# A decoder kernel with two attentions and two expert mixtures: the vector engine's first fills in 24 pieces, and one sum moved to GpSimd

## The chip, the cores and the metric

One Trainium2 chip, one of its cores. The metric is the device time of one execution in microseconds; for the kernel before it is the median of three. A core has five engines that run their own instruction streams and meet at semaphores: TensorE (PE; its weight loads are shown as PEld), the vector engine (DVE), the scalar engine (ACT), GpSimd (POOL), and SyncE (SP), which here only issues DMAs.

## The reference

The input x is 32 batches of 256 tokens by 128 channels, float32. The result is x + A(xn) + F(xn), where xn is x normalised over its channels.

```python
xn = _layernorm(x, axis=-1)
# A: attention with 16 heads of 8, rotary angles, a distance decay, causal softmax, output projection
# F: a second block on the same xn:
n1 = _layernorm(xn, ln1_w, ln1_b)
rw = _gating(n1, smha_sim, smha_gates, 2)            # 8 experts
q, k, v = einsum('btc,ech,bte->bth', n1, {q,k,v}_proj, rw)
attn_out = einsum('bth,ehc,bte->btc', softmax(q k^T / sqrt(128)) v, o_proj, rw)
hs = xn + attn_out
n2 = _layernorm(hs, ln2_w, ln2_b)
rw2 = _gating(n2, moe_sim, moe_gates, 2)
F = hs + einsum('btei,eic,bte->btc', gelu(einsum('btc,eci->btei', n2, w1)), w2, rw2)
```

What matters for the change: at the end the sum x + A + hs of a batch, called the base, is added to the second mixture's output.

## The kernel before, in words

Work is software-pipelined over the 32 batches. `step(n, u, n_x)` is written out once for every engine and holds that engine's share of step n: the second pass of attention for batch n, the maxima of batch n+1, the projections and gating of batch n+2, the first normalisation of batch n+3. `u` is the parity of n, for double buffers; `n_x` is 3 in full steps and falls to 2, 1, 0 at the end, where stages run out. Steps 0 and 1 are unrolled, then a hardware loop (`Fori(1, NB // 2 - 2)`, L1397 on DVE) runs 13 times over two steps, steps 2 to 27, and steps 28 to 31 are unrolled again. Every engine has its own loop of this kind (L517 SP, L663 POOL, L960 ACT, L1397 DVE, L1853 PE); there is no barrier between iterations, only semaphores. After step 31 a second stage follows, the mixture of `w1` and `w2` over all tokens (L1406 and after on DVE).

The order on each engine is written by hand. On DVE a step begins with `next_max(1)` (`row_max`, L1210: a row maximum over two PSUM banks, which also frees these banks for TensorE's next `unit1`), then the first two instructions of `layer_norm(n + 3)` (L1018, two `bn_stats`), a drain (L1019) and `bn_aggr` (L1021). The gating's chain of small operations follows, with more maxima between its links, then `scale_att` (L1261), `add_x` (L1268, writes `xa`), `rotate` (L1125 to L1137), and at the very end `add_hs`:

```python
                ins.then_inc(hs_done, 1)
                dve.wait_ge(hs_done, n + 1)
                dve.wait_ge(xa_done, n + 1)

                dve.wait_ge(base_stored, 16 * n)
                dve.tensor_tensor(bs[:, u], hv, xa[:, u], ALU.add).then_inc(base_done, 1)
```

Here `hs` is updated by two `scalar_tensor_tensor` (L1277) and the base is summed (L1284). SP's step n+1 begins with `wait_ge(base_done, n + 1)`, stores the base to DRAM (L474), loads `xr` for the next `add_x` (L470), spreads the gating weights (L464), and issues 24 `stk` loads (L447) and others. POOL's step holds `second_norm(n + 3)` (L643, L647), which waits for the normalisation's chain in DVE's step, and `scale(n + 1)` (L636, eight products), which waits for `max_parts` in DVE's step (L1224).

Before all this DVE writes constants: seven `memset` (L1060 to L1068), each counted on the semaphore `set_dve`. `N_FILL` is their number; SP, ACT and PE wait for that count (L414, L683, L817), and the normalisation of batch 0 follows on DVE once its x has come.

An engine's instructions stand in DRAM and are brought to it by DMA. The compiled program has 64 bytes for an instruction. Register, wait and branch instructions are among them, and count where places in the stream are given below. DVE's stream of this kernel has 437 instructions ahead of its loop (the engine's start-up apart), and the loop's body has 352. ACT's body has 107, SP's 98, POOL's 36, PE's about 1230. These counts are of the instruction records; no view prints them.

Of the kernel before, what the change touches and what calls it, by code (L numbers as in the profile page):

```python
# [10 lines left out]
ALU = mybir.AluOpType  # L11
# [4 lines left out]
S = 256  # L16
# [3 lines left out]
P = 128  # L20
T = S // P
# [104 lines left out]
def build(nc, x, w_attn, w_o, log_xi, pi_logit, e_logit, ln1_w, ln1_b, ln2_w, ln2_b, sim1, gates1,  # L126
# [9 lines left out]
    with ExitStack() as ctx:  # L136
        def sb(name, shape, dt=F32):
            return ctx.enter_context(nc.sbuf_tensor(name, shape, dt))

        def sem(name):  # L140
            return ctx.enter_context(nc.semaphore(name))
# [20 lines left out]
        ones_p = sb("ones_p", [P, P])  # L162
# [42 lines left out]
        mpart = sb("mpart", [P, T, P], BF16)  # L205
# [12 lines left out]
        hs = sb("hs", [P, NB * T, D])  # L218
        bs = sb("bs", [P, 2, T, D])
        xa = sb("xa", [P, 2, T, D])  # L220
# [85 lines left out]
        xa_done = sem("xa_done")  # L306
# [13 lines left out]
        hs_done = sem("hs_done")  # L320
        base_done = sem("base_done")
        base_stored = sem("base_stored")
# [26 lines left out]
        block = ctx.enter_context(nc.Block())  # L349
        N_CONST, N_W, N_SMALL = 8, 5, 4  # L350
        N_ROWS = 2 * NF + 2 * NF
        N_FILL = 7
        SIN_READY, N_SET_DVE = N_FILL + 11, N_FILL + 12
        UP, MOE = (2, 5, 0, 1), (4, 3)

# [22 lines left out]
        def _(sp_):  # L378
# [34 lines left out]

            sp_.wait_ge(set_dve, N_FILL)  # L414
            sp_.wait_ge(set_pool, 1)
# [175 lines left out]
        @block.gpsimd  # L591
        def _(pool):
            flat = stk[:].rearrange("p a s h t -> p a s (h t)").bitcast(F32)
            pool.memset(flat[:, 0, 0], 0.0).then_inc(set_pool, 1)
            pool.memset(flat[:, 0, 1], BF16_ONES).then_inc(set_pool, 1)
            pool.wait_ge(upper_made, 1)
            for f in range(NF):
                pool.memset(vst[:].rearrange("p a i (f g) r -> p (a i) f g r", f=NF)
                            [:, :, f, :, VO[f] + DH:VO[f] + DH + 1], 1.0).then_inc(set_pool, 1)

            def bias_rows():

                c = Chain(pool, bias_chain, 0, BIAS_LINKS)
                pool.wait_ge(ld_const, 16 * N_CONST)
                pool.wait_ge(set_act, 4)
                c.link(pool.tensor_scalar(bias_in[:, 1:2], bias_in[:, 1:2], 0.5, 0.5, ALU.mult, ALU.add))
                c.link(pool.tensor_tensor(bias_in[:, 0:1], bias_in[:, 0:1], bias_in[:, 1:2], ALU.mult))
                c.link(pool.tensor_scalar(cb[:, 0], cpos[:], bias_in[:, 0:1], None, ALU.mult))
                c.link(pool.tensor_scalar(cb[:, 1], cb[:, 0], -1.0, None, ALU.mult))
                for part in range(3):  # L610
                    c.link(pool.tensor_copy(cbp[:, :, part], cb[:]))
                    if part < 2:
                        c.link(pool.tensor_tensor(cb[:], cb[:], cbp[:, :, part], ALU.subtract))
                c.close()

            def masks():

                c = Chain(pool, mask_made, 0, 5)
                pool.wait_ge(ld_half, 16 * 4 * NF)
                for k, by in ((2, NEAR / BIG), (3, FAR / BIG), (1, FAINT)):  # L620
                    c.add(pool.tensor_scalar(mask_half[:, k], mask_half[:, k], by, None, ALU.mult))
                c.wait()
                c.add(pool.tensor_tensor(mask_r[:], mask_half[:, 3:4].broadcast_to((P, HG, P)),
                                         mask_half[:, 2:3].broadcast_to((P, HG, P)), ALU.add))
                c.add(pool.tensor_tensor(mask_l[:], mask_half[:, 1], mask_half[:, 0], ALU.add))
                c.close()

            def scale(b, par):

                pool.wait_ge(rep_in, 16 * (b + 1))  # L630
                pool.wait_ge(n1T_done, b + 1)
                pool.wait_ge(ve_out, b)
                if not isinstance(b, int) or b:
                    pool.wait_ge(max_chain, (MAX_LINKS + 1) * (b + 1))
                for e in range(E):
                    pool.tensor_tensor(n1s[:, e], rep[:, par, e], n1T[:, par], ALU.mult).then_inc(n1s_done, 1)  # L636

            def second_norm(b):

                pool.wait_ge(ln_chain, LN1_LINKS * (b + 1))  # L640
                pool.wait_ge(ln_out, b + 1)
                pool.wait_ge(xzT_out, b)
                pool.tensor_tensor(zt[:], xn[:],  # L643
                                   rstd[:, 1, 0:T].rearrange("p (i o) -> p i o", o=1).broadcast_to((P, T, D)),
                                   ALU.mult).then_inc(zp_done, 1)
                hv = hs[:, T * b:T * b + T] if isinstance(b, int) else hs[:, bass.ds(b * T, T)]
                pool.tensor_copy(hv, xn[:]).then_inc(keep_done, 1)  # L647

            def step(n, u, n_x):
                if n_x == 3:  # L650
                    second_norm(n + 3)
                if n_x:
                    scale(n + 1, 1 - u)

            second_norm(0)
            bias_rows()
            masks()
            second_norm(1)
            scale(0, 0)
            second_norm(2)  # L660
            step(0, 0, 3)
            step(1, 1, 3)
            with pool.Fori(1, NB // 2 - 2) as j:  # L663
                for u in range(2):
                    step(2 * j + u, u, 3)
            step(NB - 4, 0, 3)
            step(NB - 3, 1, 2)
            step(NB - 2, 0, 1)
            step(NB - 1, 1, 0)
# [3 lines left out]
        def _(act):  # L673
# [8 lines left out]
            act.activation(pig[:], pig[:], ACT.Tanh, scale=0.5).then_inc(set_act, 1)  # L682
            act.wait_ge(set_dve, N_FILL)  # L683
            ones = ones_p[:].rearrange("p (o t) -> p o t", o=1)
# [322 lines left out]
        def _(dve):  # L1007
# [49 lines left out]
                c.close()  # L1057

            ch = Chain(dve, set_dve, 0, N_SET_DVE)
            ch.add(dve.memset(ones_p[:], 1.0))  # L1060
            ch.add(dve.memset(ones_b[:], 1.0))
            ch.add(dve.memset(zeros_b[:], 0.0))
            ch.add(dve.memset(simx[:], 0.0))
            ch.add(dve.memset(ones_e[:], 1.0))
            ch.add(dve.memset(mpart[:], 0.0))

            ch.wait()
            ch.link(dve.memset(simx[:, 2, E:E + 1], 1.0))  # L1068
            assert ch.k == N_FILL, ch.k
            ROUND = 1.5 * 2.0 ** 23  # L1070
# [200 lines left out]
            def add_hs(n, u):  # L1271
                dve.wait_ge(oe_out, n + 1)
                dve.wait_ge(keep_done, n + 1)
                hv = hs[:, T * n:T * n + T] if isinstance(n, int) else hs[:, bass.ds(n * T, T)]
                dve.wait_ge(snorm_chain, n + 1)
                for i in range(T):
                    ins = dve.scalar_tensor_tensor(hv[:, i], ps[:, G1, i * D:(i + 1) * D], smx[:, 3, i:i + 1],  # L1277
                                                   hv[:, i], ALU.mult, ALU.add)
                ins.then_inc(hs_done, 1)
                dve.wait_ge(hs_done, n + 1)  # L1280
                dve.wait_ge(xa_done, n + 1)

                dve.wait_ge(base_stored, 16 * n)
                dve.tensor_tensor(bs[:, u], hv, xa[:, u], ALU.add).then_inc(base_done, 1)  # L1284

            def layer_norm2(g):

# [30 lines left out]
            def step(n, u, n_x):  # L1318
# [41 lines left out]
                if n_x >= 2:  # L1360
                    row_max(n + 2, 0)
                run(turn)
                add_hs(n, u)

            dve.wait_ge(set_act, 7)
# [97 lines left out]
        def _(pe):  # L1463
# [7 lines left out]
            def norm_T(b, banks, free):  # L1471

                free()
                pe.wait_ge(ln_out, b + 1)
                pe.wait_ge(zp_done, b + 1)
                for k, src in enumerate((xn[:], zt[:])):
                    for i in range(T):
                        ins = pe.transpose(ps[:, banks[0], (T * k + i) * P:(T * k + i + 1) * P], src[:, i], ident[:])
                ins.then_inc(xzT_out, 1)
# [336 lines left out]
            norm_T(0, FIRST, lambda: None)  # L1816
            pe.wait_ge(set_dve, N_FILL)
            pe.wait_ge(sim_chain, 1)
# [141 lines left out]
```

## Time and profile before

| | us |
|---|---|
| median of 3 runs (lowest, highest) | 1325.96 (1323.41, 1326.18) |
| the profiled execution | 1324.63 |
| its span | 1322.7 |
| PE busy | 1203.3 (91%) |
| DVE busy | 1034.0 (78%) |
| ACT busy | 718.8 (54%) |
| POOL busy | 222.4 (17%) |

The span is what the profile covers; 1.9 us of the execution's time lie around it. Busy times leave out waits and register instructions. "issue" in the chain of waits and as a releaser is time in which an engine waited for nothing that the profile shows.

### The profile page before, as it was taken

The page shows a single profiled execution, that of the slowest core. Times are in us where ns is not written, and L with a number is a line of the kernel's source. Part 1 is how long each engine was busy: PE and PEld are TensorE (multiplying, and loading weights), DVE is VectorE, ACT ScalarE, POOL GpSimd, SP SyncE. Part 2 cuts the span into 40 slices and gives each one's busy share as a digit, 9 for nine tenths or more (in the row PEclk, how much of TensorE's full clock was granted, in tenths as well). Part 3 has the DMA queues.
Part 4 walks back from the last instruction along what each step waited for, and adds up shares of the span by engine and source line. Part 5 has one row for each costly group of instructions (what it writes and reads, how often), then busy time and mean ns, then how long its engine had stood idle before and what let it go on. Part 6 is the DMA issues. An engine that isn't in the chain of part 4 may idle for free.

```text
span 1322.7 us, 33146 instructions
## 1 busy us (share of the span) xinstructions
PE 1203.3 (91%) x10652; PEld 917.5 (69%) x10652; DVE 1034.0 (78%) x3697; ACT 718.8 (54%) x1292; POOL 222.4 (17%) x342
## 2 busy tenths in 40 slices
PE   2599989898989898989898979898999989999998
PEld 1377767676767676767676757676787767777776
DVE  8899969696969696969696969696997577777664
ACT  4166646464646464646464646464656865555532
POOL 4112111111111111111111211121231100000000
PEclk9899989897989897989898989898999999999999
DMA  4533322322222222222222222222233144444453
GB/s 106 147 107 107 91 87 81 83 81 82 80 83 82 82 82 82 80 84 82 82 81 82 82 81 82 82 82 82 83 93 91 38 149 161 161 161 161 162 195 140
DMA packets 103172, 133.50 MB, mean 101 GB/s; under 512 B 13576, under 2 KB 82424, under 8 KB 94864
## 3 DMA queue, kind: packets, MB, share of 16 engines
q1 hardware_dynamic: 100548, 130.72, 31.9%
q10 hardware_dynamic: 2508, 1.58, 0.5%
q14 instruction: 85, 0.70, 0.2%
q8 instruction: 31, 0.51, 0.2%
HBM read 109.12 MB, written 21.54 MB: 99 GB/s over the span
## 4 chain that ended last, share of the span: by engine, by line
PE 52%; DVE 27%; issue 17%; DVEq 2%; ACT 1%; DMA 1%; ACTq 1%; POOL 0%; SPq 0%; POOLq 0%
PE ps L1890 8%; PE ps L1876 8%; PE ps L1613 5%; PE ps L1623 4%; PE ps L1659 4%; PE ps L1614 4%; DVE mx L1210 3%; PE ps L1590 3%; PE ps L1486 2%; DVE rots L1129 2%; PE ps L1539 1%; PE ps L1549 1%; PE ps L1573 1%; DVE rots L1126 1%; DVE rots L1135 1%
## 5 line engine op out<-in xcount | busy, mean ns | idle before, releaser
L1210 DVE TENSOR_REDUCE mx<-ps 128x4 f32<-128x1024 f32 (+1 forms) x192 | 234.9, 1223 | 80.0 <-PE ps L1549 33.1
L779 ACT ACTIVATE pr<-ps 128x1024 f32<-128x1024 f32 x192 | 196.6, 1024 | 170.3 <-PE ps L1573 104.4
L636 POOL TENSOR_TENSOR n1s<-rep,n1T 128x256 f32<-128x256 f32 x256 | 177.3, 730 | 323.8 <-DVE mpart L1224 307.1
L785 ACT ACTIVATE ps<-trn 128x1024 f32<-128x1024 bf16 x191 | 196.5, 1029 | 5.1
L1613 PE MATMUL ps<-n1s,wqk 128*128 128x256 f32 x512 | 180.0, 436 | 0.0
L1890 PEld LDWEIGHTS ps<-w2s,ats 128*128 128x128 f32 x1024 | 131.4, 191 | 52.7 <-issue 43.9
L1614 PE MATMUL ps<-n1s,wqk 128*128 128x256 f32 x512 | 166.3, 409 | 0.0
L979 ACT ACTIVATE n1s<-ps 128x512 f32<-128x512 f32 x128 | 76.6, 598 | 121.0 <-PE ps L1876 119.9
L1890 PE MATMUL ps<-w2s,ats 128*128 128x128 f32 x1024 | 136.0, 276 | 2.4 <-DVE ats L1414 2.4
L1623 PE MATMUL ps<-wv,n1s 128*128 128x128 f32 x1024 | 133.1, 278 | 0.0
L1876 PE MATMUL ps<-rep,w1s 128*128 128x512 f32 x256 | 130.7, 594 | 0.0
L1623 PEld LDWEIGHTS ps<-wv,n1s 128*128 128x128 f32 x1024 | 124.3, 192 | 4.9
L1659 PE MATMUL ps<-wop,ats 128*128 128x128 f32 x1024 | 126.4, 276 | 0.0
L1659 PEld LDWEIGHTS ps<-wop,ats 128*128 128x128 f32 x1024 | 119.6, 192 | 5.6 <-issue 2.9
L1614 PEld LDWEIGHTS ps<-n1s,wqk 128*128 128x128 f32 x512 | 107.0, 209 | 17.6
L1613 PEld LDWEIGHTS ps<-n1s,wqk 128*128 128x128 f32 x512 | 96.5, 210 | 28.4 <-issue 18.0
L643 POOL TENSOR_TENSOR zt<-xn,rstd 128x256 f32<-128x256 f32 x32 | 20.5, 642 | 492.6 <-DVE rstd L1038 492.6
L1261 DVE TENSOR_TENSOR ats<-rep,ps 128x512 f32<-128x512 f32 (+1 forms) x160 | 81.1, 572 | 0.0
L732 ACT ACTIVATE n1T<-xzT,lnp 128x256 f32<-128x256 f32 x32 | 19.2, 600 | 110.3 <-POOL n1s L636 110.3
L1590 PE MATMUL ps<-pr,vst 128*32 128x256 f32 x1024 | 74.2, 411 | 0.6 <-ACT pr L779 0.6
L1539 PE MATMUL ps<-mask_r,mask_l 64*128 64x256 bf16 x256 | 37.2, 287 | 40.5 <-DVE mx L1210 40.5
L1539 PEld LDWEIGHTS ps<-mask_r,mask_l 64*128 64x128 bf16 x256 | 12.3, 93 | 71.0 <-DVE mx L1210 54.3
(229 smaller groups left out, 2074.9 us busy)
## 6 DMA issues: line engine op xcount, KB each, us to landing
rep<-scr_rw SPq DMA_DIRECT2D x32, 1024.0 KB, 5.7
stk<-scr_rw SPq DMA_DIRECT2D x16, 1024.0 KB, 8.6
scr_parts<-parts SPq DMA_DIRECT2D x64, 192.0 KB, 5.8
stk<-scr_parts SPq DMA_DIRECT2D x248, 48.0 KB
rots<-scr_rw SPq DMA_DIRECT2D x8, 1024.0 KB, 4.7
wqk<-scr_rw SPq DMA_DIRECT2D x8, 1024.0 KB, 9.1
stk<-scr_parts SPq DMA_DIRECT2D x248, 32.0 KB
xt<-in_x SPq DMA_DIRECT2D x32, 128.0 KB, 2.2
```

Source lines behind the costliest of these rows:

```text
L636: pool.tensor_tensor(n1s[:, e], rep[:, par, e], n1T[:, par], ALU.mult).then_inc(n1s_done, 1)
L779: act.activation(pr[:, Q, :, i], ps[:, S2[0]:S2[0] + NF], ACT.Exp).then_inc(exp_done, 1)
L785: act.activation(ps[:, S2[0]:S2[0] + NF], seeds[:, kind:kind + 1].broadcast_to((P, NF, 512)), ACT.Copy).then_inc(seed_done, 1)
L1210: dve.tensor_reduce(mx[:, min(i, 1)].rearrange("p (f h) -> p f h", f=NF)[:, :, h:h + n], ps[:, S1[0]:S1[0] + NF].rearrange("p f (h t) -> p ...
L1261: dve.tensor_tensor(ats[:, e:e + ne], rep[:, u, e:e + ne], ps[:, G0:G0 + 1, 0:S].broadcast_to((P, ne, S)), ALU.mult).then_inc(ats_done, 1)
L1590: mm(ps[32 * h:32 * h + 32, PVB, 0:S], vst[:, u, 0, HH * f + HG * Q + h], pr[:, Q, f, h // 2, (h % 2) * S:(h % 2 + 1) * S], start=(f == 0) ...
L1613: mm(ps[:, QKB, 0:S], wq[:, e], n1s[:, e], start=(e == 0), stop=(e == E - 1), skip_group_check=True)
L1614: ins = mm(ps[:, QKB, S:2 * S], wk[:, e], n1s[:, e], start=False, stop=(e == E - 1), skip_group_check=True)
L1623: ins = mm(ps[:, QKB, i * D:(i + 1) * D], n1s[:, e, i * P:(i + 1) * P], wv[:, e], start=(e == 0 and i == 0), stop=(e == E - 1), skip_group ...
L1659: ins = mm(ps[:, G1, i * D:(i + 1) * D], ats[:, e, i * P:(i + 1) * P], wop[:, e], start=(e == 0 and i == 0), stop=(e == E - 1), skip_group ...
L1876: mm(ps[:, UP[k % 4]], w1s[:, e], n2T[t % 8], start=True, stop=True).then_inc(up_out, 1)
L1890: ins = mm(ps[:, MOE[t % 2], i * D:(i + 1) * D], hgs[:, k % 2, i * P:(i + 1) * P], w2s[:, e], start=(e == 0 and i == 0), stop=(e == E - 1) ...
```

## The change

The fill of `ones_p` becomes 16 `memset` of 8 columns each, that of `mpart` 8 `memset` of 32 elements a row each, so that `N_FILL` is 29 in place of 7. The base's sum leaves DVE's `add_hs` and becomes `add_base` at the end of GpSimd's step, with the same three waits. What is computed stays the same. In the words that came with it, DVE's loop then begins at instruction 455 of its stream.

```diff
-        N_FILL = 7
+        FILLS_ONES, FILLS_MAX = 16, 8
+        N_FILL = 5 + FILLS_ONES + FILLS_MAX
...
+            def add_base(n, u):
+
+                pool.wait_ge(hs_done, n + 1)
+                pool.wait_ge(xa_done, n + 1)
+                pool.wait_ge(base_stored, 16 * n)
+                hv = hs[:, T * n:T * n + T] if isinstance(n, int) else hs[:, bass.ds(n * T, T)]
+                pool.tensor_tensor(bs[:, u], hv, xa[:, u], ALU.add).then_inc(base_done, 1)
+
             def step(n, u, n_x):
                 if n_x == 3:
                     second_norm(n + 3)
                 if n_x:
                     scale(n + 1, 1 - u)
+                add_base(n, u)
...
-            ch.add(dve.memset(ones_p[:], 1.0))
+            for k in range(FILLS_ONES):
+                ch.add(dve.memset(ones_p[:, k * P // FILLS_ONES:(k + 1) * P // FILLS_ONES], 1.0))
             ch.add(dve.memset(ones_b[:], 1.0))
             ch.add(dve.memset(zeros_b[:], 0.0))
             ch.add(dve.memset(simx[:], 0.0))
             ch.add(dve.memset(ones_e[:], 1.0))
-            ch.add(dve.memset(mpart[:], 0.0))
+            mparts = mpart[:].rearrange("p i h -> p (i h)")
+            for k in range(FILLS_MAX):
+                ch.add(dve.memset(mparts[:, k * S // FILLS_MAX:(k + 1) * S // FILLS_MAX], 0.0))
...
                 ins.then_inc(hs_done, 1)
-                dve.wait_ge(hs_done, n + 1)
-                dve.wait_ge(xa_done, n + 1)
-
-                dve.wait_ge(base_stored, 16 * n)
-                dve.tensor_tensor(bs[:, u], hv, xa[:, u], ALU.add).then_inc(base_done, 1)
```

## Rows read from the trace of the kernel before

**Rows 1.** The page: span; chain by engine; instruction DMA queues (packets, MB).
```profile
span 1322.7 us, 33146 instructions
...
q14 instruction: 85, 0.70, 0.2%
q8 instruction: 31, 0.51, 0.2%
...
PE 52%; DVE 27%; issue 17%; DVEq 2%; ACT 1%; DMA 1%; ACTq 1%; POOL 0%; SPq 0%; POOLq 0%
```

**Rows 2.** DVE's waits: line, releaser: us in total, times, longest.
```profile
DVE bmv L1021 <- issue: 52.6, 12, 4.8
...
DVE mx L1210 <- issue: 32.5, 12, 3.0
```

**Rows 3.** The chain of waits across one back jump of DVE's loop: start, us, what.
```profile
640.63 0.06 DVEq L1397
640.69 2.76 issue
643.45 0.09 DVEq L1397
...
644.73 0.47 DVE bst L1018 x2
645.20 3.97 issue
649.18 0.16 DVEq L1019
```

**Rows 4.** DVE's loop instruction: all its branches.
```profile
L1397 DVEq COMPARE_BRANCH  x13: 55/63/72, 179.2 to 969.2; - x13
```

**Rows 5.** Steps by window, the odd ones' sum last: us, busy PE, PEld, DVE, ACT, POOL, PEclk.
```profile
122.20:150.88 28.68, 28.41 (x286) 22.59 (x285) 26.11 (x94) 18.61 (x33) 6.51 (x10) 1.00 0.34 96
150.88:179.14 28.26, 27.84 (x282) 21.85 (x281) 26.11 (x94) 17.54 (x33) 6.49 (x10) 1.00 0.35 96
...
640.54:677.50 36.96, 31.63 (x285) 24.25 (x284) 26.28 (x95) 18.57 (x33) 6.52 (x10) 0.91 0.26 73
677.50:705.76 28.26, 27.84 (x283) 21.97 (x282) 26.26 (x95) 17.69 (x33) 6.49 (x10) 1.00 0.35 95
...
sum 450.86, PE 383.19 PEld 292.57 DVE 315.87 ACT 223.30 POOL 78.42; mean PE 31.93 PEld 24.38 DVE 26.32 ACT 18.61 POOL 6.54
```

**Rows 6.** Instruction DMAs in windows 122.2:179.1 (two rows), 640.5:706, 640.5:643.5 and 645.2:649.4.
```profile
q8 instruction: 5, 0.08, 0.6%
q14 instruction: 5, 0.04, 0.3%
...
q14 instruction: 5, 0.04, 0.2%
...
q14 instruction: 1, 0.01, 1.0%
...
q14 instruction: 1, 0.01, 0.5%
```

**Rows 7.** DVE in order of time at the end of a step without a jump.
```profile
676.76 0.61 DVE L1277 SCALAR_TENSOR_TENSOR hs<-ps,smx,hs 128x128 f32 x2
677.50 0.42 DVE L1284 TENSOR_TENSOR bs<-hs,xa 128x256 f32<-128x256 f32 x1
677.84 1.22 DVE L1210 TENSOR_REDUCE mx<-ps 128x4 f32<-128x1024 f32 x1
```

**Rows 8.** PE in order of time: waits for that maximum; then slow after a jump.
```profile
679.11 0.28 PE L1539 MATMUL ps<-mask_r,mask_l 64*128 64x256 bf16 x2 [0.31 <-DVE mx L1210]
...
644.87 0.28 PE L1539 MATMUL ps<-mask_r,mask_l 64*128 64x256 bf16 x2 [2.70 <-DVE mx L1210]
...
645.81 1.22 PE L1613 MATMUL ps<-n1s,wqk 128*128 128x256 f32 x2
```

**Rows 9.** GpSimd's product, and two equal DVE products, the first beside it.
```profile
L636 POOL TENSOR_TENSOR n1s<-rep,n1T 128x256 f32<-128x256 f32 x256 | 177.3, 730 | 323.8 <-DVE mpart L1224 307.1 <-DMA rep<-scr_rw 16.8
...
L1129 DVE TENSOR_TENSOR rots<-rots,cs 128x512 f32<-128x512 f32 x32 | 30.8, 963 | 1.1
L1130 DVE TENSOR_TENSOR rots<-rots 128x512 f32<-128x512 f32 x32 | 22.1, 692 | 1.1
```

**Rows 10.** SP's and GpSimd's waits in the window 677.5 to 706.
```profile
SPq L474 <- DVE bs L1284: 8.0, 1, 8.0
...
POOL zt L643 <- DVE rstd L1038: 13.5, 1, 13.5
```

**Rows 11.** DVE's first instructions in order of time.
```profile
0.82 0.17 DVE L1060 MEMSET ones_p<- 128x128 f32 x1 [0.82 <-PEq L1954]
...
1.45 0.07 DVE L1064 MEMSET ones_e<- 128x8 f32 x1
1.49 0.17 DVE L1065 MEMSET mpart<- 128x128 uint32 x1
...
3.05 0.48 DVE L1018 BATCH_NORM_STATS2 bst<-xt 128x6 f32<-128x128 f32 x2 [1.27 <-DMA xt<-in_x]
```

## The prediction

> **What bounds the kernel now.** I read the page first: TensorE and DVE carry the chain, but 17% of it is "issue", time in which nothing is shown to be waited for [rows 1]. The view of DVE's waits puts this in one place. The `bn_aggr` of the first normalisation and the maximum `mx` wait for "issue" 12 times each, 52.6 and 32.5 us [rows 2]. DVE's loop branches 13 times and jumps back 12 times [rows 4]. The chain of waits across one jump shows both: after the branch 2.76 us of nothing, the maximum and two `bn_stats`, then 3.97 us of nothing before the drain [rows 3].
>
> The steps fall into two kinds [rows 5]. The 12 that begin with a jump take 450.86 us together, 37.57 each; the others of the same form take 28.26. The difference, 9.31 us, is 6.7 us of the two gaps and the rest TensorE's: it waits 2.70 us for the maximum and then runs a pair of products in 1.22 us where it takes about 0.6 otherwise [rows 8], and the granted clock of such a step is 0.91 against 1.00 [rows 5], a part of it at 1.2 in place of 2.4 GHz.
>
> The gaps are instruction fetches. In each a packet of an instruction queue starts, and five come in the 65 us of an iteration [rows 6]; 85 packets are 0.70 MB [rows 1], so a packet is 8 KB, at 64 bytes 128 instructions. The body of 352 instructions needs 3 to 4 such blocks; five packets an iteration mean that all of it, and the block after it, is fetched anew each time.
>
> **Where the block's edges are.** The second gap stands before the drain, the eighth instruction of the body. With 437 ahead of the loop an edge lies after 444 of them, the next at 572, 700 and 828. The body before, 437 to 788, so touches four blocks, 7 instructions in the first. Entering a block starts the fetch of the next (in straight stretches packets come once per 128 instructions, with no gap). So five are wanted in one turn, and when DVE jumps back the first is gone.
>
> How many are kept? The first turn, window 122.2 to 179.1, has 5 packets on q14 and 5 on q8, which is TensorE's with 16 KB each [rows 1, 6]. By count 3 of the 5 on q14 are DVE's, one each ACT's and SP's, whose bodies of 107 and 98 have an edge inside. In a later turn q8 has none and q14 only DVE's five [rows 6]. ACT and SP thus keep at least 3 blocks of 8 KB (two touched, one ahead), and TensorE, whose body touches six, at least 7 of 16 KB. DVE fails with 5. The case of 4 is not shown.
>
> **The change part by part.** *The place.* 24 fills stand for 2, which is 22 more; the two unrolled steps ahead of the loop lose the sum and one wait instruction each, 4 fewer: 437 + 22 - 4 = 455, as the change says. The body has at most 352, so it lies in 455 to 806, between the edges 444 and 828, with 11 and 22 to spare: three blocks and one ahead, 4 in all. I take it that four are kept, since an engine that keeps three and fails at five sits by a power of two at four, and because TensorE keeps seven or more of the larger. Then no jump fetches, and a step with a jump is as long as one without. Steps 1, 2 and 3 ran in sequence with no jump between them in 28.68 and 28.26 us [rows 5], so the 28.26 is no catching-up after a stall. The gain is 450.86 - 12 x 28.26 = 111.7 us. Bounds: nothing, and 111.7.
>
> *The sum's removal from DVE.* In a step without a jump the sum starts at 677.50 and the next maximum at 677.84; the last `hs` update ends at 677.37 [rows 7]. DVE's queue is shorter by 0.47 us a step. TensorE, though, is busy 27.84 of 28.26 us, and waits for DVE's maximum 0.31 us [rows 5, 8]. It has no more to give: of the 0.47, 0.31 a step, over 29 steps 9.0 us. What is late next is TensorE's own stream. In the last three steps DVE is not the one waited for. Bounds: 0, and 29 x 0.47 = 13.6 us.
>
> *The sum on GpSimd.* No row shows this operation there. The nearest is its product of two operands of the same 128x256, 0.73 us [rows 9]. It runs after `scale`, when the next work of that engine is 13.5 us away behind the normalisation [rows 10], so nothing queues behind it: `second_norm(n + 4)` and `scale(n + 2)` both wait for DVE's next step. The store of the base comes about 0.4 us later, and with it in SP's queue the `xr` load, the weights' spread and the `stk` loads. SP waits 8.0 us there in a full step [rows 10], which hides it. Cost 0; without that cover 0.4 x 31 = 12 us. The other price is DVE beside GpSimd: its product L1129 takes 0.963 us on average, the equal L1130, with GpSimd quiet, 0.692 [rows 9]. The sum would run beside the maximum and `bn_stats`; I take 0, with 0.27 x 31 = 8 us as the upper bound, and 0 below.
> The Trainium skill ("SBUF — State Buffer", section "SBUF: two separate sides") has a DVE operation with two SBUF inputs locked out for the whole of a GpSimd operation. L1129 agrees in direction. By that rule an overlap with such an operation would cost 0.73 us a step, 23 us in all; the maximum (from PSUM) and `bn_stats` have one input, and by the same rule go free.
>
> *The fills.* The narrowest fill seen, 8 columns, took 0.07 us, the wide ones 0.17 [rows 11]. 24 at 0.07 to 0.17 are 1.7 to 4.1 us in place of 0.33. The x of batch 0 leaves 1.27 us idle before the first `bn_stats` [rows 11], so at 0.08 each (nearest to the narrow row) it is 1.9 - 0.3 - 1.3, some 0.3 us late; ACT's clearing of `vst`, which waits for the count, may follow. I take 1 us; bounds 0 and 3.
>
> *Sum*, against the profiled execution's 1324.63 (span 1322.7 and 1.9 around it): 1324.6 - 111.7 - 9.0 + 0 + 1.0 = 1204.9. The median of the runs is 1.3 above that execution, so 1206; with half of the unknown delays beside GpSimd (2 us) I forecast 1208.
>
> **The rivals.** *A: fewer than four blocks are kept.* The jump still misses, but the next block is fetched during the 117 instructions that remain in the first. The gap of 3.97 goes with what follows it; the first gap stays, 2.70 us of TensorE's wait and some 1.6 us of slow products after it. Per jump 4.3 in place of 9.31, 12 x 5.0 = 60 us: 1324.6 - 60 - 9 + 1 + 1.3 = 1258. For it: the four is not shown. Against: it would leave three. Chance 0.07.
> The Trainium skill ("Runtime: NRT & Kernel Launch", section "Instruction fetch mechanics") speaks for A: only two lines of 16 KB, and a taken branch out of them stops for a fetch. Here q14's packets are 8 KB and come one by one, and ACT keeps three, so the trace does not bear out its size of line; its total of 32 KB would be four of 8 KB, which is my forecast.
>
> *B: after a jump that misses, the next block is asked for only when the stream reaches the edge.* Then, if A's condition holds too, the gap of 3.97 just moves 117 instructions on: 1324.6 - 9 + 1 + 1.3 = 1318. For it: the second packet starts after DVE has stopped at the drain. Against: edges elsewhere cost nothing. Chance 0.05.
>
> *C: the base comes too late for SP* (slower). Place: L474, at the head of SP's step. Price 0.4 to 0.5 us a step, 14 us over 31, if SP's wait of 8.0 us were used up; it counts as slower only where the jumps keep their price: 1326 + 14 = 1340. Against: that wait. Chance 0.02.
>
> *D: the change doesn't do what it says*: the edges lie elsewhere than I count and the body still has four blocks and a short first one, DVE's shorter queue alone remaining and eaten by GpSimd's sum: about 1325. Against: the drain's place and 455 agree to the instruction. Chance 0.02.
>
> **How the numbers follow.** The forecast has 0.84. Its own range: low 1196 with DVE's full 0.47 a step and no cost for the fills (1326.0 - 111.7 - 13.6 = 1200.7, and 5 for products that follow sooner), high 1225 with TensorE's 0.31 not gained and 8 us beside GpSimd (1326.0 - 111.7 + 8 + 3). It holds 19 of 20 of that case, 0.80 in all, so it reaches to no rival. Faster by over 0.2% (2.7 us, about what a measurement of this kernel can tell from no change): the forecast, A and B, 0.96. Within 0.2%: D, 0.02. Slower: C, 0.02.
>
> **What would show it.** Right: no "issue" rows at the head of the loop for L1210 and L1021; no q14 packets in the middle of the loop and about 60 fewer than 85 in all; every full step near 28.0 us at a clock of 1.00; TensorE's wait for `mx` gone from steps of both kinds; a GpSimd `bs` of 0.6 to 0.8 us; L474 waiting for it with several us left. Wrong: five q14 packets an iteration still and one gap at the branch (A); a second gap some 117 instructions after the jump (B); DMAs of `stk` awaited by TensorE (C). Should steps stay at 28.26 without jumps' gaps, then only the term of 9 us was wrong.

## The result and the profile after

| | before | after |
|---|---|---|
| median of 4 runs on one chip, us (lowest, highest) | 1326.07 (1323.41, 1329.04) | 1211.95 (1211.61, 1212.19) |
| ratio, with its 95% interval | 1 | 0.9139 [0.9119, 0.9158] |
| span of the profiled execution, us | 1322.7 | 1210.4 |
| granted clock, mean of that execution | 0.958 | 0.994 |

The kernel is 114 us faster, 8.6%. The forecast of 1208 was 4 us short of it, and 1211.95 lies in its range.

The page of the kernel after: span, busy time, two instruction queues, and the chain that ended last. It answers to [rows 1].

```profile
span 1210.4 us, 33207 instructions
...
PE 1161.8 (96%) x10652; PEld 896.3 (74%) x10652; DVE 1018.8 (84%) x3687; ACT 717.7 (59%) x1292; POOL 245.9 (20%) x374
...
q8 instruction: 31, 0.51, 0.2%
q14 instruction: 26, 0.21, 0.1%
...
PE 77%; DVE 14%; issue 6%; ACT 1%; ACTq 1%; DVEq 1%; DMA 1%; POOL 0%; SPq 0%; POOLq 0%
```

Queue q14 carries 26 packets in place of 85, q8 (TensorE's) the same 31 as before. "issue" falls from 17% of the chain to 6%, and TensorE holds 77% of it in place of 52%. DVE's largest waits (line, releaser: us in total, times, longest) now all name TensorE; the two "issue" rows of [rows 2] are gone.

```profile
DVE ats L1422 <- PE ps L1898: 66.4, 73, 2.3
DVE mx L1223 <- PE ps L1557: 20.7, 36, 1.7
DVE xa L1281 <- PE ps L1681: 16.1, 29, 0.6
```

The loop still runs 13 times and jumps back 12 times, as in [rows 4]:

```profile
L1405 DVEq COMPARE_BRANCH  x13: 50/56/67, 178.1 to 855.5; - x13
```

DVE in order of time across the jump at 403.91 (start, us, instruction), to set beside [rows 3]. The maximum follows the last `hs` update at once, and the `bn_aggr` follows `bn_stats`: neither gap is left.

```profile
404.05 0.60 DVE L1290 SCALAR_TENSOR_TENSOR hs<-ps,smx,hs 128x128 f32 x2
404.56 1.22 DVE L1223 TENSOR_REDUCE mx<-ps 128x4 f32<-128x1024 f32 x1
405.69 0.47 DVE L1028 BATCH_NORM_STATS2 bst<-xt 128x6 f32<-128x128 f32 x2
406.24 0.25 DVE L1031 BATCH_NORM_AGGREGATE bmv<-bst 128x2 f32<-128x6 f32 x2
```

Three steps by window, from one end of `hs` to the next, the first with that jump (columns as in [rows 5]). A step with a jump is as long as one without, at a clock of 1.00, and TensorE is busy for all but 0.11 to 0.13 us of it. TensorE's waits for DVE's maximum, 40.5 us in 29 cases and 33.9 in 13 before, are 2.8 in 4 and 2.6 in one.

```profile
404.91:433.15 28.24, 28.11 (x284) 22.30 (x283) 25.53 (x94) 18.16 (x33) 7.26 (x11) 1.00 0.33 95
433.15:461.36 28.21, 28.10 (x284) 22.27 (x283) 25.92 (x94) 18.05 (x33) 7.24 (x12) 1.00 0.33 95
461.36:489.57 28.21, 28.09 (x284) 22.23 (x283) 25.48 (x94) 18.10 (x33) 7.26 (x12) 1.00 0.33 95
```

From the ends of `hs` in both traces the difference closes. The first comes 0.4 us later (93.99, 94.39). The 12 steps with a jump take 338.7 us in place of 449.7, and the 19 others together 2.4 us less. What follows the last is 0.7 us longer (245.5, 246.2). 0.4 - 111.0 - 2.4 + 0.7 = -112.3, which is the difference of the spans.

### The profile page after: what moved, and what is told of

It is laid out like the page before. It is cut to its first block, busy times and chain, and to the rows that moved or that the text cites. A ratio compares the mean times of both kernels' runs of the same rounds, so it can differ in the third digit from the quotient of the medians.

```text
span 1210.4 us, 33207 instructions
## 1 busy us (share of the span) xinstructions
PE 1161.8 (96%) x10652; PEld 896.3 (74%) x10652; DVE 1018.8 (84%) x3687; ACT 717.7 (59%) x1292; POOL 245.9 (20%) x374
## 4 chain that ended last, share of the span: by engine, by line
PE 77%; DVE 14%; issue 6%; ACT 1%; ACTq 1%; DVEq 1%; DMA 1%; POOL 0%; SPq 0%; POOLq 0%
PE ps L1621 10%; PE ps L1667 10%; PE ps L1898 9%; PE ps L1622 9%; PE ps L1884 9%; PE ps L1631 5%; PE ps L1494 3%; PE ps L1598 3%; PE ps L1581 2%; PE ps L1557 2%; PE ps L1547 2%; PE ps L1544 2%; DVE att L1249 1%; PE ps L1554 1%; PE ps L1603 1%
## 5 line engine op out<-in xcount | busy, mean ns | idle before, releaser
L1621 PE MATMUL ps<-n1s,wqk 128*128 128x256 f32 x512 | 164.7, 404 | 1.3 <-issue 1.3
L1622 PE MATMUL ps<-n1s,wqk 128*128 128x256 f32 x512 | 153.8, 382 | 0.0
L1622 PEld LDWEIGHTS ps<-n1s,wqk 128*128 128x128 f32 x512 | 98.4, 192 | 13.8
L1621 PEld LDWEIGHTS ps<-n1s,wqk 128*128 128x128 f32 x512 | 89.3, 195 | 26.0 <-issue 15.9
L742 ACT ACTIVATE n1T<-xzT,lnp 128x256 f32<-128x256 f32 x32 | 19.2, 600 | 108.2 <-POOL n1s L637 108.2
L1598 PE MATMUL ps<-pr,vst 128*32 128x256 f32 x1024 | 68.5, 385 | 0.6 <-ACT pr L789 0.6
L656 POOL TENSOR_TENSOR bs<-hs,xa 128x256 f32<-128x256 f32 x32 | 23.3, 728 | 200.2 <-DVE hs L1290 200.2
L1422 DVE TENSOR_TENSOR ats<-n1s,stk 128x512 f32<-128x512 f32 x64 | 44.0, 688 | 14.0 <-PE ps L1898 13.9
```

The lines of the kernel that those rows point to most:

```text
L1598: mm(ps[32 * h:32 * h + 32, PVB, 0:S], vst[:, u, 0, HH * f + HG * Q + h], pr[:, Q, f, h // 2, (h % 2) * S:(h % 2 + 1) * S], start=(f == 0) ...
L1621: mm(ps[:, QKB, 0:S], wq[:, e], n1s[:, e], start=(e == 0), stop=(e == E - 1), skip_group_check=True)
L1622: ins = mm(ps[:, QKB, S:2 * S], wk[:, e], n1s[:, e], start=False, stop=(e == E - 1), skip_group_check=True)
```

## The experiments

All runs stand in one table; ratios are against runs of the kernel before on the same chip. "Left" is how many instructions of the body lie in the block it begins in, by edges after 444, 572, 700 and 828. "Second packet" is when, after a branch that misses, the second instruction packet starts, as a mean over 12 jumps; it is from the trace's packet records, which no view prints. Steps run from one end of `hs` to the next, means over the loop without its first step. A blank means that it does not apply.

| run | sum on | loop, first to last | left | q14 | second packet, us | step with jump | other | median, us | ratio [95%] |
|---|---|---|---|---|---|---|---|---|---|
| before | DVE | 437-788 | 7 | 85 | 7.12 | 37.48 | 28.36 | 1326.07 | 1 |
| after | GpSimd | 455-801 | | 26 | none | 28.23 | 28.20 | 1211.95 | 0.9139 [0.9119, 0.9158] |
| fills_only | DVE | 459-810 | | 26 | none | 28.48 | 28.36 | 1217.85 | 0.9175 [0.9156, 0.9195] |
| sum_only | GpSimd | 433-779 | 11 | 85 | 3.58 | 30.99 | 28.22 | 1246.97 | 0.9399 [0.9374, 0.9424] |
| head_437 | GpSimd | 437-783 | 7 | 85 | 3.71 | 31.71 | 27.97 | 1251.12 | 0.9441 [0.9416, 0.9466] |
| head_443 | GpSimd | 443-789 | 1 | 85 | 3.71 | 35.40 | 27.94 | 1295.41 | 0.9753 [0.9726, 0.9779] |
| head_444 | GpSimd | 444-790 | | 25 | none | 28.34 | 28.09 | 1211.66 | 0.9129 [0.9106, 0.9152] |
| head_481 | GpSimd | 481-827 | | 26 | none | 28.22 | 28.22 | 1212.08 | 0.9139 [0.9117, 0.9161] |
| head_483 | GpSimd | 483-829 | 89 | 86 | (text) | 32.57 | 28.23 | 1264.21 | 0.9530 [0.9504, 0.9556] |
| dve_443 | DVE | 443-794 | 1 | 86 | 7.16 | 39.87 | 28.35 | 1354.20 | 1.0214 [1.0189, 1.0239] |
| rep_late | DVE | 437-788 | 7 | 85 | 4.03 | 32.85 | 28.35 | 1269.50 | 0.9586 [0.9564, 0.9608] |
| rep_sooner | GpSimd | 437-783 | 7 | 85 | 7.10 | 36.95 | 27.97 | 1314.44 | 0.9931 [0.9908, 0.9954] |
| pe_less | GpSimd | as after | | 26 | none | 28.21 | 28.17 | 1211.13 | 0.9153 [0.9131, 0.9174] |
| seven_experts | GpSimd | as after | | 26 | none | 27.93 | 27.93 | 1204.72 | 0.9085 [0.907, 0.910] |

### The two parts apart

fills_only takes the fills of the change and leaves the sum on DVE (against the kernel before, the fills' loops as in the change):

```diff
-        N_FILL = 7
+        FILLS_ONES, FILLS_MAX = 16, 8
+        N_FILL = 5 + FILLS_ONES + FILLS_MAX
```

> The 24 fills alone, the base's sum left on DVE: DVE's loop then begins after 459 instructions and its 352 end at 810, three blocks. Theory W (DVE keeps four blocks of 128 instructions, the one fetched ahead included, edges after 444, 572, 700 and 828): no fetch in the loop, steps of 28.2 to 28.3 us, 1212 to 1214 us, the whole gain. Theory S (the sum's move carries a part of the gain worth the forecast's 9 us): 1219 to 1222 us, steps of 28.5 us. A theory that the gain is the sum's alone would have 1326 us.

sum_only takes the sum's move and leaves the fills whole (on the kernel after):

```diff
-        FILLS_ONES, FILLS_MAX = 16, 8
+        FILLS_ONES, FILLS_MAX = 1, 1
```

> The sum on GpSimd alone, the seven fills as before: the loop begins after 433 and ends at 779, four blocks, 11 instructions in the first. Theory W: five packets an iteration as before, a first gap of 2.6 to 3 us at the jump and a second of 4 us some 11 instructions on; 1323 to 1327 us. Theory S: 1317 us, since DVE's queue is 0.47 us a step shorter.

The fills alone bring 108.2 us, to 1217.85, and all gaps are gone (109.4 us by the ratio to the kernel before in the same set of runs). Behind them the sum's move is worth another 5.9 us (4.8 by the ratios). The second run was the surprise. With the loop at 433, in the wrong place, its queue has 85 packets as before, and yet it takes 1247, not about 1326; neither theory had that. Its page and DVE's waits:

```profile
q14 instruction: 85, 0.70, 0.2%
...
DVE mx L1223 <- issue: 27.1, 12, 2.4
```

The gap at the branch is still there (before: 32.5). The row for `bn_aggr`, 52.6 us in [rows 2], is not. Both parts therefore work against the same loss, and their gains don't add: 108 and 79 alone, 114 together.

### Where the edges are

All four on the kernel after, and only the number of fills differs:

```diff
-        FILLS_ONES, FILLS_MAX = 16, 8
+        FILLS_ONES, FILLS_MAX = 8, 4      # head_443
+        FILLS_ONES, FILLS_MAX = 8, 5      # head_444
+        FILLS_ONES, FILLS_MAX = 40, 10    # head_481
+        FILLS_ONES, FILLS_MAX = 40, 12    # head_483
```

> As the changed kernel, but with 12 fills for two: the loop begins after 443, one instruction ahead of the edge that I count, and ends at 789. Theory W: four blocks are touched and the jump misses: both gaps, steps with a jump of 37 to 38 us, 1323 to 1328 us. Theory D (what counts is only how far the loop's head is from where it was, or the count of fills): near 1212 us.

> One more fill: the loop begins after 444, with the first instruction of a block, and ends at 790. Theory W: three blocks, no fetch in the loop, 1211 to 1212 us, some 115 us less than with the loop one instruction earlier. If the edge lies elsewhere by an instruction or two, 1325 us.

> 50 fills for two, the sum on GpSimd: the loop begins after 481 and its 347 instructions end at 827, the branch the last of the third block. Theory W (four blocks of 128, the one ahead included): no fetch in the loop, 1212 to 1214 us (a microsecond or two of it the fills). A theory that DVE reads some instructions ahead of the branch and so enters a fourth block: 1240 us or more.

> 52 fills for two: the loop ends at 829, two instructions into a fourth block. Theory W: entering it fetches the fifth, the first is gone, and every jump misses: five packets an iteration. With 89 instructions left in the first block the second fetch is covered: one gap of 2 to 3 us a jump, steps with a jump of 30.5 to 31.5 us, 1240 to 1250 us. A theory of three blocks and the branch's own place not counting: 1213 us.

One memset more or less, 443 against 444, is worth 84 us: 1295.41 and 1211.66. The edge is where theory W had it. Its price for the miss, 1323 to 1328 us, is some 30 us too high, as it was by nearly 80 us for sum_only. Below, DVE's waits of head_443:

```profile
DVE mx L1223 <- issue: 58.6, 12, 5.3
```

At the other end, a body whose last instruction is number 827 needs no fetch, and with 829 it needs one in each iteration. The pages of head_481 and head_483, and the second one's wait:

```profile
q14 instruction: 26, 0.21, 0.1%
```

```profile
q14 instruction: 86, 0.70, 0.2%
...
DVE mx L1223 <- issue: 39.7, 12, 3.5
```

So a body in three blocks, with one block ahead, stays; a body that touches a fourth does not. The edges are where the prediction had them, and the four is shown. In the iteration from 403.9 to 460.4 of the kernel after there is no packet on q14 at all, not even for the block ahead. head_483 is also rival A's picture: a jump that misses with 89 instructions left. It takes 1264 us where 1240 to 1250 were expected: the one gap is 3.3 us, not 2 to 3. Its packets start at 0.69, 1.12 and 7.89 us after the branch. The branch lies two instructions into its fourth block, so I take the first of them to be the block ahead, still on its way, which holds up the one that is wanted; no run shows that. There is no second gap.

### What sets the price of a jump that misses

sum_only left this open: the place was as bad as before and the price a third. head_437 puts the loop of the kernel after exactly where it was before; dve_443 moves the loop of the kernel before by six instructions, to where head_443 has it.

```diff
-        FILLS_ONES, FILLS_MAX = 16, 8
+        FILLS_ONES, FILLS_MAX = 5, 1      # head_437
...
-        N_FILL = 7
+        FILLS_ONES, FILLS_MAX = 6, 2      # dve_443, sum stays on DVE
+        N_FILL = 5 + FILLS_ONES + FILLS_MAX
```

> The sum on GpSimd and 6 fills for two: the loop begins after 437 as before the change, 7 instructions ahead of the edge, the drain first behind it. The run with 11 ahead of the edge lost 2.7 us a jump, the kernel before with 7 lost 9.3, the one with 1 ahead 7.4. Theory P (the place decides): the second packet comes 7 us after the branch, a gap of 4 us at the drain, steps with a jump of 37 us, 1317 to 1325 us. Theory Q (the sum in DVE's queue is what delays the second fetch in the kernel before): second packet 3.5 us after the branch, steps of 31 to 34 us, 1250 to 1290 us.

> The sum on DVE and 8 fills for two: the loop begins after 443, one instruction ahead of the edge. Theory P: as the run with the sum on GpSimd at the same place, steps with a jump 7 to 8 us longer than the others, second packet 3.5 us after the branch; with the 6 us that the sum on DVE costs, 1300 us. Theory Q: a second packet 7 us after the branch and steps of 37 us, 1325 us.

At one place the sum's engine makes 75 us: 1251 at 437 against 1326, and 1295 at 443 against 1354, 59 us. dve_443 is slower than before, by 28 us, although nothing but small fills was added. Theory Q had the time of head_437 and the second packet of both. For dve_443 both theories' times, 1300 and 1325, were too low. The two blocks of dve_443 are both awaited in one gap at the head:

```profile
DVE mx L1222 <- issue: 102.9, 13, 9.0
```

and of head_437 (two groups, at the places of [rows 2]):

```profile
DVE mx L1223 <- issue: 27.8, 12, 2.5
DVE bmv L1031 <- issue: 13.5, 12, 1.5
```

The first gap hardly changes (2.3 us each, before 2.7). The second is 1.1 us each in place of 4.4. The packet records say why: after the branch the first packet starts at 1.0 to 1.1 us in the mean of each of these runs (head_483 apart), the second at 3.4 to 4.4 in the runs with the sum on GpSimd and at 6.8 to 7.6 with it on DVE. What else moves between them is SP. It waits for the base and then issues the stores, and among them the spread of the gating weights, `rep`, 1 MB. The timelines of SP in before (branch at 575.14) and head_437 (branch at 593.19) show the issue 1.9 and 3.0 us after the branch:

```profile
577.07 0.37 SPq L464 DMA_DIRECT2D rep<-scr_rw  x1
```

```profile
596.20 0.37 SPq L465 DMA_DIRECT2D rep<-scr_rw  x1
```

Most of this shift is in the branch, not in SP. In the kernel before DVE waits for its own `hs` ahead of the sum, and so branches after the updates; without that wait it branches first. The updates in before and in head_437, to set beside the branches at 575.14 and 593.19:

```profile
574.42 0.60 DVE L1277 SCALAR_TENSOR_TENSOR hs<-ps,smx,hs 128x128 f32 x2
```

```profile
593.32 0.60 DVE L1290 SCALAR_TENSOR_TENSOR hs<-ps,smx,hs 128x128 f32 x2
```

Counted from the end of `hs`, the branch comes 0.9 us sooner in head_437, and with it the first fetch; the spread comes 0.2 us later.

If the second packet waits behind that transfer, moving the transfer must move the price. Each of the two runs moves a little more than the transfer: rep_late issues the 192 KB stores of `scr_parts` earlier and the `stk` loads later, rep_sooner takes the 128 KB load of `xr` along. rep_late is the kernel before with the spread held back (until `lg_read` counts n + 3); rep_sooner is head_437 with the spread ahead of the wait for the base:

```diff
+                if late:                  # rep_late: in spread_weights
+                    sp_.wait_ge(lg_read, b + 2)
...
-                    spread_weights(n + 1, 1 - u)
+                    spread_weights(n + 1, 1 - u, n_x >= 2)
...
+                sp_.wait_ge(hs_done, n)   # rep_sooner: then x and the spread, and only then
...
                 sp_.wait_ge(base_done, n)
                 if not isinstance(n, int) or n > 0:
                     store_base(n - 1, 1 - u)
```

> The kernel before, but SP's 1 MB spread of the gating weights (rep) is issued after the parts' store and only once DVE has read the next gating's logits, some 7 us later in a step. Theory K (after a jump that misses, the second block is asked for about 3.4 us after the branch, and in the kernel before that packet stands behind the rep transfer, which fills the DMA engines from 2.5 to 8 us): second packet near 3.5 us after the branch, a gap of about 1 us at the drain in place of 4, steps with a jump of 31 to 33 us, 1255 to 1270 us. Theory L (what delays it is the sum or its wait in DVE's own queue): unchanged, second packet at 7 us, 1324 to 1328 us.

> The run with the sum on GpSimd and the loop at 437 (1251 us), but SP waits for DVE's hs, not for the base, ahead of the xr load and the rep spread, and stores the base behind them: the rep transfer starts as soon after the branch as in the kernel before (issued at about 1.7 us in place of 3.0), while DVE's queue stays without the sum. Theory K: second packet at 6.5 to 7.5 us, the gap of 4 us at the drain is back, steps with a jump of 36 to 38 us, 1315 to 1325 us. Theory L: 1250 to 1255 us.

Both went the way of theory K: rep_late is 54 us faster than the kernel before in the same set of runs (1269.50 against 1323.27), rep_sooner 63 us slower than head_437. The branches are at 547.76 and 503.23; the spread now starts 11.9 and 1.4 us after them:

```profile
559.62 0.33 SPq L466 DMA_DIRECT2D rep<-scr_rw  x1
```

```profile
504.67 0.37 SPq L465 DMA_DIRECT2D rep<-scr_rw  x1
```

The chain of waits after each branch, rep_late and then rep_sooner. The first gap is of one kind, the second 1.17 us in the one and 4.29 in the other (4.06 at the jump of before at 575):

```profile
547.83 2.69 issue
...
551.80 0.48 DVE bst L1020 x2
552.27 1.17 issue
```

```profile
503.96 2.04 issue
...
507.28 0.48 DVE bst L1029 x2
507.75 4.29 issue
```

And the DMA engines between 3.4 and 6.8 us after the branch, when the second block is wanted. Last columns: granted clock, DMA share, GB/s; before, rep_late, rep_sooner, head_437:

```profile
578.54:581.94 3.40, 2.42 (x18) 1.94 (x19) 1.32 (x3) 1.62 (x2) 0.00 (x0) 0.76 0.96 270
```

```profile
551.16:554.56 3.40, 2.62 (x22) 1.96 (x22) 1.98 (x11) 1.82 (x2) 0.00 (x0) 1.00 0.22 64
```

```profile
506.63:510.03 3.40, 2.61 (x22) 1.96 (x22) 1.12 (x3) 1.81 (x2) 0.00 (x0) 1.00 0.95 280
```

```profile
596.59:599.99 3.40, 2.49 (x20) 2.08 (x21) 2.18 (x11) 1.69 (x2) 0.00 (x0) 0.86 0.96 289
```

In head_437 the engines are as full as in before; there the spread's issue comes at 3.0 us, and the packet starts at 3.5 (3.7 in the mean), just ahead of most of it. So it is not the share alone but which of the two is first. By these runs the second block is asked for about 3.5 us after the branch. If 1 MB was issued 1.4 to 1.9 us after the branch, the packet starts only at about 7.1.

### What bounds a step after the change

pe_less drops the product that adds the causal mask to the second attention's scores; seven_experts drops the eighth expert from the values of the second attention.

```diff
-                mm(b.rearrange("p (a t) -> p a t", a=2)[:, :, 0:P], identb[:], mask_qk[:, 0:2], start=True,
-                   stop=False, skip_group_check=True)
-                mm(b[:, 0:P], qT[:, 0:P], kT[:, 0:P], start=False, stop=True, skip_group_check=True)
+                mm(b[:, 0:P], qT[:, 0:P], kT[:, 0:P], start=True, stop=True, skip_group_check=True)
...
-                             start=(e == 0 and i == 0), stop=(e == E - 1), skip_group_check=True)
+                             start=(e == 0 and i == 0), stop=(e == E - 2), skip_group_check=True)
...
-                for e in range(4, E):
+                for e in range(4, E - 1):
```

> The changed kernel without the mask's product in the second attention's scores (the causal mask is left out there, one TensorE matmul of 0.21 us in each of the 32 steps). Theory T (a step is TensorE's stream, end to end, so that DVE's shorter queue gave only what it did): 0.21 us less a step, 1205 to 1206 us. Theory V (DVE's own chain bounds the step): 1211 to 1212 us.

> The changed kernel with the eighth expert left out of the second attention's values: four TensorE products (0.43 us from the start of one group to that of the next) fewer in each of 32 steps. The mask's product, left out before, had moved the products behind it by 0.04 us only, so that run could not tell the theories apart. Theory T (a step is TensorE's stream): 0.43 us less a step, 1198 to 1199 us. Theory V (DVE's chain bounds the step, and TensorE only fills it): 1210 to 1212 us. Between, some 1203 us, DVE's next wait takes over when TensorE is 0.2 us shorter.

pe_less landed on theory V's 1211, but it tells nothing. The products behind the dropped one came only 0.04 us sooner, and TensorE's busy time fell by 1.8 us in all, 0.06 a step, not 0.21. A step went from 28.20 to 28.17 us, and the intervals of 0.9139 and 0.9153 overlap. seven_experts takes more: TensorE's busy time falls by 15.8 us, 0.49 a step. The steps fall by 0.27 to 0.30 us (28.20 and 28.23 to 27.93 in the means), and the run by 7.2. That is between theories T and V, near the 1203 that was expected if DVE's next wait took over. A window of 28 us and the wait that appears:

```profile
432.00:460.00 28.00, 27.62 (x283) 21.85 (x280) 26.18 (x94) 18.09 (x33) 7.22 (x11) 1.00 0.32 96
```

```profile
PE ps L1675 <- DVE att L1249: 9.4, 32, 0.6
```

That last wait was 2.1 us in 5 cases in the kernel after, and is 9.4 in 32 here, 0.29 each. So TensorE's own stream set the step after the change, and DVE's chain, at some 27.9 us, was 0.3 us shorter.

## Why the prediction was right, and where it wasn't

**The place (-111.7): right in mechanism, 3.5 us too large.** Fills alone bring 108.2 by the medians. The prediction gave a step with a jump, once its fetches are gone, the 28.26 us of the steps that follow one. Between starts of the sum, as in [rows 5], fills_only has 28.57 and 28.27 by turns, the first with the jump, and 12 x (37.57 - 28.57) = 108.0. The first step of a turn of the loop is thus the longer one even without fetches. The 28.68 us in [rows 5], of the loop's first step and without a jump, had shown it. What makes it longer is not shown. With the shorter queue it is hidden (between ends of `hs`, 28.23 against 28.20).

**Four blocks are kept: right.** It was the unshown step, and went by analogy (ACT and SP keep three, TensorE seven), so that it came out was in part luck: no row told four from three. The pairs 443/444 and 827/829 show it to within two instructions. The Trainium skill ("Runtime: NRT & Kernel Launch", section "Instruction fetch mechanics") has a taken branch out of the lines held stop for a fetch; the runs agree, 12 jumps with q14 packets and a gap or 12 without. Its two lines of 16 KB do not fit: packets are 8 KB, four are held, and only the sum of 32 KB agrees.

**The sum off DVE (-9.0): right in sign, half as large again as measured.** Measured 5.9 by medians (1217.85 - 1211.95), 4.8 by the ratios (0.9175 and 0.9139, each uncertain by 0.002), so 0.16 to 0.20 us over 29 steps in place of 0.31. The mis-sized quantity is TensorE's spare time. The 0.31 us of waiting for the maximum and "busy 27.84 of 28.26 us" were read in a step that follows a jump. No records are missing there: the page counts 10652 products before and after, and two steps in a row have 285 and 283 in [rows 5], 284 and 284 in after. In the step after a jump TensorE has less to do, since a part of its work has run in the step before. Steps without fetches and with the sum still on DVE are those of fills_only. There TensorE waits for the maximum L1222 only 6.7 us in 10 cases in the whole run, and between starts of the sum it has:

```profile
293.06:321.63 28.57, 28.27 (x284) 22.41 (x283) 26.08 (x95) 18.27 (x33) 6.54 (x10) 1.00 0.33 94
321.63:349.89 28.26, 28.02 (x283) 22.13 (x283) 26.20 (x95) 17.88 (x33) 6.49 (x10) 1.00 0.34 95
```

The spare time there is 0.24 to 0.30 us a step, of which 0.11 to 0.13 stays after the change. What is late next is TensorE's own stream, as said.

**The sum on GpSimd (0): right.** The operation took 0.728 us, and its line waits for DVE only. SP waits for it 175 us in 32 steps, before 208.8. In two full steps of after that is 5.2 and 4.4 us, where [rows 10] have 8.0. The product of DVE that had run slow beside GpSimd is no slower now, 0.896 against 0.963 us [rows 9].

```profile
L656 POOL TENSOR_TENSOR bs<-hs,xa 128x256 f32<-128x256 f32 x32 | 23.3, 728 | 200.2 <-DVE hs L1290 200.2
...
L1142 DVE TENSOR_TENSOR rots<-rots,cs 128x512 f32<-128x512 f32 x32 | 28.7, 896 | 1.1
```

```profile
SPq L475 <- POOL bs L656: 175.0, 32, 23.3
```

The 2 us set aside for delays beside GpSimd found no trace: the maximum in the timeline above takes 1.22 us, as in [rows 7]. The Trainium skill ("SBUF — State Buffer", section "SBUF: two separate sides") has GpSimd lock out a DVE operation only if that has two SBUF inputs or runs in a 2-port perf mode. The maximum, which reads PSUM, went free beside the sum, and this agrees.

**The fills (+1.0): too high, about 0.** 16 pieces took 0.49 us and 8 took 0.24, so one costs 0.03 us where I took 0.08: the 0.07 of [rows 11] is the duration of a single one, so in a row they must overlap. The first normalisation starts at 2.95 (3.05 before) and still waits 0.80 us for x.

```profile
0.80 0.49 DVE L1071 MEMSET ones_p<- 128x8 f32 x16 [0.80 <-PEq L1962]
...
1.78 0.24 DVE L1078 MEMSET mpart<- 128x16 uint32 x8
...
2.95 0.48 DVE L1028 BATCH_NORM_STATS2 bst<-xt 128x6 f32<-128x128 f32 x2 [0.80 <-DMA xt<-in_x]
```

Added up: 3.5 and 3.1 us of gain too much, 1.0 of cost too much and 2.0 for the unknown set against it, leaves 3.6 us; the miss was 4.0.

**The rivals.** A did not come; had it, its 1258 would have been near: head_483, the nearest to it that ran, takes 1264. B did not come, and where a jump misses, the second block is not left until DVE stands at the edge: in head_437, at the branch of 593.19, its packet starts 3.5 us after it, when DVE is in the maximum (596.22 to 597.46 in its trace), two `bn_stats` ahead of the drain, and head_483 has no second gap at all. C did not come; SP's wait has 4 to 5 us left in a full step. D was wrong as stated, whatever its chance: with the place still bad, the sum's move does not end at about 1325 but at 1247 to 1251 (sum_only, head_437). I had taken the price of a jump that misses, 9.31 us, for a property of the place. The runs show a race on the DMA side between the second packet and the spread. Moving the sum off DVE puts the spread's issue 1.1 us later after the branch, mostly because DVE branches sooner, and that is enough for the packet to win.

## What to carry to other kernels

"issue" at the head of a loop, as often as the loop jumps, is its instructions being fetched again: count the stream's instructions, find the edges from where the second gap stands, and shift the loop until it fits in three blocks of 128; a few cheap instructions ahead of it can be worth 8% here, and any edit that adds instructions ahead can lose them again. Where a loop can't fit, keep bulk transfers from being issued in the first 3 us after the jump. A shorter queue on an engine is worth what the bounding engine has spare, and that is not to be read in a step that follows a stall: compare the count of its instructions with that of its neighbours.

## What the runs showed of the hardware

- DVE keeps four blocks of 8 KB (128 instructions), the one ahead among them. A body that ends at 827 stays, one that ends at 829 is fetched anew in each iteration.
- A jump that misses cost 2.8 us (sum_only), 3.7 (head_437), 4.3 (head_483), 4.5 (rep_late), 7.5 (head_443), 9.0 (rep_sooner), 9.1 (before) and 11.5 (dve_443), each as step with a jump less another step. With 11, 7 and 1 instructions left in the first block it rises from 2.8 to 3.7 and 7.5, and with bulk traffic ahead of the second packet from 3.7 to 9.0 at the same place.
- An instruction packet did not pass data that was issued before it: the 1 MB spread, issued 1.4 to 1.9 us after the branch, held it to 7.1 us; issued at 3.0 or 11.9 it let the packet start at 3.7 or 4.0. That it is this transfer is shown by moving it, once later and once sooner, with little else moved; by which rule of the queues it holds the packet up stays open.
- The runs with longer gaps on DVE have a lower granted clock on TensorE: 0.958 in before, 0.982 in rep_late and 0.994 in after, as means of the profiled executions. In the 3.4 us windows above it was 0.76 in before, so part of the time at 1.2 in place of 2.4 GHz, and 1.00 in rep_late, though TensorE had been busy for 1.56 and 1.55 us of the 3.4 us ahead of them.
